# Causal attention on one Trainium2 core: probability-by-value products in three groups a pair, a place of its own for each unit's probabilities, and expert matrices loaded later

## The reference, cut to what matters

```
qc = jnp.einsum('bthd,dl->bthl', q, Wc)
att = jnp.einsum('bthl,bshl->bhts', qc, k) * SCALE
causal = jnp.tril(jnp.ones((Tv, Tv), dtype=bool))
att = jnp.where(causal[None, None], att, -jnp.inf)
att = jax.nn.softmax(att, axis=-1)
y = jnp.einsum('bhts,bshl->bthl', att, v).reshape(Bv, Tv, N_HEAD * LATENT)
```

```
h = jnp.einsum('te,td,edf->tf', onehot, xn, W1) + b1[idx]
y = jnp.einsum('te,tf,efd->td', onehot, h, W2) + b2[idx]
```

## Time and profile before

| what | value |
|---|---|
| median of 3 runs | 3310.96 us (3310.6 to 3314.94) |
| the profiled execution's own time | 3309.64 us |
| its span, first to last instruction | 3307.9 us |
| granted TensorE clock, mean | 0.924 |
| causal pairs (`attend_pairs`), PE's instructions | about 1395.6 to 2125 us |

### The profile page before, as it was taken

One profiled execution on the slowest core, in us unless ns is written; L12 is line 12 of the kernel. 1 busy time (PEld: TensorE's weight loads), 2 busy tenths in 40 slices (PEclk: granted clock), 3 DMA queues, 4 the chain that ended last, 5 costly groups with the idle time before them and its releaser, 6 DMA issues. The chain is left out here.

```text
span 3307.9 us, 49216 instructions
## 1 busy us (share of the span) xinstructions
PE 2539.1 (77%) x12725; PEld 1095.9 (33%) x12907; DVE 2463.3 (74%) x4022; ACT 1835.5 (55%) x3590; POOL 1192.3 (36%) x1612
## 2 busy tenths in 40 slices
PE   5797699999998698589999999686834555555575
PEld 4543122222222543134444444285620111111454
DVE  6667788888885667787777777265368999999843
ACT  1212488888887111135555555403328999999532
POOL 1013433333331212258888888802640000000154
PEclk9799799999999599789999999896978999999688
DMA  5002322222222202622222222151121111110012
GB/s 174 0 0 68 87 72 76 77 71 76 76 71 67 76 0 80 228 66 68 78 79 81 78 70 81 56 182 45 42 90 52 33 33 32 32 32 29 9 52 80
DMA packets 183846, 223.37 MB, mean 68 GB/s; under 512 B 55088, under 2 KB 104496, under 8 KB 183216
## 3 DMA queue, kind: packets, MB, share of 16 engines
q1 hardware_dynamic: 144000, 192.41, 18.0%
q0 software_dynamic: 29696, 23.27, 2.9%
q10 hardware_dynamic: 9968, 5.51, 0.6%
HBM read 136.67 MB, written 83.76 MB: 67 GB/s over the span
## 5 line engine op out<-in xcount | busy, mean ns | idle before, releaser
L1101 DVE TENSOR_REDUCE neg_max<-ps 128x1 f32<-128x1024 f32 x512 | 602.4, 1220 | 89.1 <-PE ps L989 88.4
L1474 POOL TENSOR_TENSOR acc<-acc,prob 128x512 f32<-128x512 f32 (+3 forms) x640 | 578.3, 944 | 99.0 <-PE ps L1318 99.0
L1068 ACT ACTIVATE prob<-ps 128x512 f32<-128x512 f32 x1024 | 556.3, 602 | 87.6 <-PE ps L1003 74.2
L1903 DVE TENSOR_REDUCE neg_max<-ps 128x1 f32<-128x1024 f32 x512 | 579.3, 1209 | 5.4 <-PE ps L1886 5.4
L1926 ACT ACTIVATE ps<-ps,neg_max 128x1024 f32<-128x1024 f32 x512 | 557.2, 1088 | 9.7 <-DVE neg_max L1903 9.7
L1886 PE MATMUL ps<-k_stack,q_stack 128*128 128x512 bf16 x992 | 303.8, 386 | 291.5 <-ACT ps L1926 273.6
L1398 ACT ACTIVATE prob<-ps 128x512 f32<-128x512 f32 (+3 forms) x640 | 266.3, 477 | 258.4 <-PE ps L1302 126.9
L1443 DVE TENSOR_REDUCE neg_max<-ps 128x1 f32<-128x128 f32 (+7 forms) x512 | 388.1, 758 | 17.5
L1003 PE MATMUL ps<-q_stack,k_stack 128*128 128x512 bf16 x946 | 292.6, 386 | 6.9 <-ACT prob L1068 4.6
L1013 PE MATMUL ps<-prob,v 128*32 128x512 f32 x2048 | 280.6, 620 | 3.6 <-ACT prob L1068 0.7
L1441 DVE TENSOR_TENSOR ps<-ps,mask_qk 128x128 f32<-128x128 f32 x512 | 151.1, 295 | 157.5 <-PE ps L1275 157.0
(11 more groups left out here) (292 smaller groups left out, 3877.0 us busy)
## 6 DMA issues: line engine op xcount, KB each, us to landing
q_stack<-q_parts SPq DMA_DIRECT2D x576, 48.0 KB
k_stack<-k_parts SPq DMA_DIRECT2D x576, 48.0 KB
o_quads<-o_out SPq DMA_DIRECT2D x64, 256.0 KB
v_heads<-v_out SPq DMA_DIRECT2D x4, 4096.0 KB
v<-v_heads SPq DMA_DIRECT2D x32, 512.0 KB
o_pairs<-o_out SPq DMA_DIRECT2D x64, 256.0 KB, 5.8
num<-o_pairs SPq DMA_DIRECT2D x8, 2048.0 KB
q_parts<-parts SPq DMA_DIRECT2D x24, 384.0 KB
```

Source lines behind the costliest of these rows:

```text
L1068: nc.scalar.activation(prob[:, m % RING, :], ps[:, bank(m), :], ACT.Exp).then_inc(exped.sem, 1)
L1101: nc.vector.tensor_reduce(neg_max[:, i.slot(2), m:m + 1], ps[:, first:first + 2, :].rearrange("p b n -> p (b n)"), AX.X, ALU.max, negate=T ...
L1474: nc.gpsimd.tensor_tensor(sums, sums, weights(j, u, h), ALU.add).then_inc(added.sem, 1)
L1903: nc.vector.tensor_reduce(neg_max[:, i.slot(2), qt:qt + 1], ps[:, 2 * (qt % 4):2 * (qt % 4) + 2, :], AX.XY, ALU.max, negate=True).then_inc ...
```

## The change

The change has three parts. PE's loop over couples goes in steps of two: the six groups of 8 instructions become three groups of 16, W4 with W5 of pair i - 3, W0 with W1, and W2 with W3 of pair j; second and first scores that stood between them are put behind each group. The ring `prob` grows from 5 places to 10, one for each unit, and ACT's waits follow from that. The expert matrices are taken from the list of early loads and are loaded at the start of the first `route_best`, on SP, ahead of its stores.

```diff
-    RING = 5
+    RING = NU - FIRST
...
-                    for k in range(COUPLES):
+                    for k in range(0, COUPLES, 2):
                         if two:
                             for t in range(4 * k, 4 * k + 3):
                                 second_scores(j, t, n)
                         if one:
                             first_scores(i, next(pieces))
                         if k == 0 and there(n, 3):
+                            weigh(i - 3, COUPLES - 2)
                             weigh(i - 3, COUPLES - 1)
                         if k > 0 and two:
+                            weigh(j, k - 2)
                             weigh(j, k - 1)
-                        if one and k < NQ - 2 * COUPLES:
+                        if one and k == 0:
                             first_scores(i, next(pieces))
-                        if two:
-                            second_scores(j, 4 * k + 3, n)
-                        if one:
-                            first_scores(i, next(pieces))
-                        if k == 1 and there(n, 1):
+                        for t in range(4 * k + 3, 4 * k + 8):
+                            if two:
+                                second_scores(j, t, n)
+                            if one and t > 4 * k + 3:
+                                first_scores(i, next(pieces))
+                        if k == 0 and there(n, 1):
                             turn_shift(i - 1, n)
-                        if k == 3 and there(n, 3):
+                        if k == 2 and there(n, 3):
                             sum_up(i - 3, n)
...
-                                    elif u - RING >= FIRST:
-                                        pv_mm.wait(act, j.times(2 * NU, 2 * (u - RING) + h))
-                                        added.wait(act, j.times(ADDS, 2 * (u - FIRST - RING) + h))
                                     elif n != 2:
-                                        pv_mm.wait(act, (j - 1).times(2 * NU, 2 * (u + RING) + h))
-                                        added.wait(act, (j - 1).times(ADDS, 2 * (u - FIRST + RING) + h))
+                                        pv_mm.wait(act, (j - 1).times(2 * NU, 2 * u + h))
+                                        added.wait(act, (j - 1).times(ADDS, 2 * (u - FIRST) + h))
...
             @block.sync
             def _(sp):
+                for dst, src in S.expert_loads:
+                    sp.dma_start(dst, src).then_inc(experts_loaded, 16)
                 for g in range(GROUPS):
                     sp.wait_ge(normed2, g + 1)
...
-        S.f1_w1, S.f1_b1 = weight("f1_w1", [P, E * 4 * P]), row("f1_b1")
-        S.f1_w2, S.f1_b2 = weight("f1_w2", [P, E * 4 * P]), row("f1_b2")
```

More of the change, by code:

```diff
@@ L2066, in route_best @@
             "normed transposed copied xT_ready l_mm").split()]
+        experts_loaded = sem("experts_loaded")
         with nc.Block() as block:
@@ L2104, in _ @@
                 sp.wait_ge(x_stored, 16 * GROUPS)
+                if S.expert_loads:
+                    sp.wait_ge(experts_loaded, 16 * len(S.expert_loads))
             @block.gpsimd
@@ L2394, in _, with expert_weights @@
                     sp.wait_ge(out_stored, 16 * GROUPS)
+def expert_weights(nc, S, a, ctx):
+    S.f1_w1 = ctx.enter_context(nc.sbuf_tensor("w_f1_w1", [P, E * 4 * P], F32))
+    S.f1_b1 = ctx.enter_context(nc.sbuf_tensor("w_f1_b1_row", [P, E * 4 * P], F32))
+    S.f1_w2 = ctx.enter_context(nc.sbuf_tensor("w_f1_w2", [P, E * 4 * P], F32))
+    S.f1_b2 = ctx.enter_context(nc.sbuf_tensor("w_f1_b2_row", [P, E * P], F32))
+    S.expert_loads = [(S.f1_w1[:], a["f1_w1"]), (S.f1_b1[:], a["f1_b1"].partition_broadcast(P)),
+                      (S.f1_w2[:], a["f1_w2"]), (S.f1_b2[:], a["f1_b2"].partition_broadcast(P))]
 def best_expert_ffn(nc, S, out=None):
@@ L2406, in best_expert_ffn @@
         route_best(nc, S)
+        S.expert_loads = []
         expert_tiles(nc, S, out)
@@ L2490, in program @@
         for layer in layers:
+            if layer is best_expert_ffn:
+                expert_weights(nc, S, a, ctx)
             layer(nc, S)
```

## The result

The changed kernel takes 3390.31 us (median of 4 runs, 3386.6 to 3394.92) against 3311.9 us (3310.6 to 3314.94). The ratio is 1.0236, with a 95% interval of 1.0218 to 1.0254: slower by 78 us. The forecast was 3374 us, within 3345 to 3400. The profiled execution took 3388.84 us.

A forecast was written before the change was run, and what follows sets the result against it. PE's list was taken to set the pace in the causal pairs, with short waits for DVE and ACT. 3309.64 + 63.1 = 3372.7 us profiled, the median 1.3 us higher: 3374 us, range 3345 to 3400.

The forecast's parts named there:

- The walk: Causal pairs: four engine lists timed through one step; 21.78 us a round before, 23.75 us after, 1.97 us longer.
- Waits for DVE: PE's waits ahead of f3, f5, f9, f14, f15, with f4's 0.08: 4.36 us a round, 3.69 more than before.
- POOL's wait: Sign in the profile after: POOL's wait for W0 in a round at 5.2 us.
- Fewer groups save 0.33 us each: Part 1, PE in a pair: three of six changes of kind go, 0.99 us less of PE's own work.
- rival C: Fixed 0.33 us belongs to each couple, so nothing is saved: 24.74 us a round, 3405 us; chance 6%.
- The loss is PE's wait for DVE: Causal pairs: bunched first scores make PE wait 4.36 us for DVE; wrong if waits stay below 1.7 us a pair.
- Rival B: No change: longer DVE waits (3.69) come to about half, savings pay for them; within 7 us of 3311; chance 3%.
- Places and loads at 0: Parts 2 and 3: ten `prob` places give 0 by themselves; late expert loads cost 0, 3 us at the high end.
- five places do not do in the new order: Part 2: with five places s18's exponential would have waited for W2, so ten are needed, giving 0 by themselves.
- The layer's start and end: Causal pairs: the starting round adds 1.0 us, the last three steps 4.9 us, within 63.1 us together.
- rival D: PE's work share falls to 79% and its clock with it: 60 us on top, 3434 us or more; chance 2%.
- Rival A: Score work between groups stays hidden, only three changes of kind count: -32 us, 3279 us; chance 6%.

## Why the prediction was right, point by point

- **The walk.** Forecast: a round of 23.75 us. Measured: 23.78. Waits for DVE: forecast 1.07, 1.03, 0.74, 0.56 and 0.88 us; by the page, with 0.17 added, 1.05, 1.02, 0.73, 0.55 and 0.86. Groups: forecast 3.4, 2.6 and 2.4 us; measured 3.43, 2.61 and 2.37. DVE idle ahead of f7: forecast 3.0, measured 2.93. POOL's wait: forecast 5.2, measured 5.21 to 5.23 at full clock.
- **Fewer groups save 0.33 us each.** Right: seen in the lengths of the groups, and shown by cutting couples, 0.35 us for each change added. This also answers rival C (the cost belongs to each couple), which needed a round of 24.74 us.
- **The loss is PE's wait for DVE.** Shown from two sides: with half of DVE's work the orders are equal within 1 us, and with other places for the first scores the groups of sixteen lose nothing against the kernel before. Rival B (half of the longer waits) fell with it: the waits came as forecast.
- **Places and loads at 0.** Right, 0.0% with an interval of 0.1%. The loads ran at 427 and 400 GB/s from 2312 to 2318 and 2318 to 2324 us, and DMA was idle again when the stores began at 2333.61. My sentence that five places do not do in the new order was too strong: the kernel ran with five at the same time. It holds for other orders only: in the list of the run with three groups, s21 stands ahead of W2, and by the walk it would wait there for ever with five places, which was not tried.
- **The layer's start and end.** 63.1 us forecast for the pairs; 63.8 us without the long rounds. About 8 us of either lie outside the 28 full rounds.
- **The term that was missing.** Of the 16 us between forecast and result, 13.0 are the stretches at the lower clock, 2.4 lie behind the layer and 0.7 are the walk's. With them the result stands at the upper end of the forecast's own range of 3355 to 3390 us; the stated range held it because it had been widened for rival C, and not for the clock. Filling the waits took 12 us off, which confirms the size. This was rival D, which I gave 2% and set aside because the row attention holds full clock with PE busy for 105 of 200 us. That row was no evidence for this place. A mean over 200 us says nothing of how the idle time is spread, and here four of five waits fall into two bunches. D priced a slow tenth of every round, 60 us and more; what came were six of 28 rounds with some 2 us more, 13 us.
- **Rival A** (only the changes of kind count, 3279 us) fell. It would have needed waits under 1.7 us in sum; they are 4.2. The Trainium skill's rule on tiling modes ("TensorEngine Tiling (Array Packing)", Key Properties) says that a change of mode drains the engine. The runs agree that each change costs something, 0.33 to 0.35 us here; they do not tell the mode from the change of type between bf16 and float32. That price does not decide the time where another engine holds PE up.

What stays open: why the clock falls in six of the 28 rounds, though all rounds hold the same waits. That filling the waits ahead of f3 and f5 is enough to stop it is shown; what picks the round is not. The first two pairs of long rounds start 195 us apart with ten places and with five, but from 1702 us on in one kernel and from 1751 us on in the other. The 1.1 us behind the sums lie in the later layers and were not traced.

## What to carry to other kernels

When an in-order engine feeds a second one through two buffers, count for each long group what the second engine has in hand when it begins; a group longer than that makes it idle, and if the work for it then comes in a bunch, the first engine waits. Here the second engine was idle 2.93 us at one group, though it was busy for only 135.5 of 200 us, and the first one waited 4.2 us a round. Before merging groups to save switches, try the order of the feeding instructions with the groups as they are: here that gave 47 us, with the same instructions. Writing down the engines' lists for one round with durations of the trace, and demanding that it give the round of before to 0.1 us, was enough to forecast four new orders to 0.4 us a round, three of them to 0.1; the clock has to be asked for apart.

## What the runs showed of the hardware beyond what was expected

- Idle pieces of 0.4 to 0.9 us, in a list that is otherwise dense, were enough for TensorE's clock to be granted at 1.2 GHz for 6.8 and 3.4 us in two rounds on end, six of 28 rounds in all (PE busy 167 of 200 us in a stretch ahead), and 30 products of 128 columns in two of these pieces kept it at 2.4 GHz (busy 184 of 200 us). The kernel became 12 us faster by doing more work.
- A change from score products (bf16) to prob by v products (float32, 64 columns of the array) and back cost PE 0.33 to 0.35 us, in groups merged and in couples cut.
- The same kernel holds full clock with PE busy for 105 of 200 us in the row attention, so the mean busy share of a stretch does not tell whether the clock falls.
